# First layer in two stages with the norms inside, and the attention half of the joined scan stage issued by steps for all batches

## The reference

```python
# _layernorm: (x - mean) / sqrt(var + 1e-5)
x = x + L0_attn(_layernorm(x))        # layer 0
#   h = layernorm(x)*g1 + b1; q,k,v = h@wq, h@wk, h@wv; phi = elu + 1
#   kv = sum_s phi(k) v ; z = sum_s phi(k)
#   x = x + (phi(q) kv / (phi(q) z + 1e-6)) @ wo
#   h = layernorm(x)*g2 + b2
#   x = x + lookup(h @ w1) @ w2
#   lookup(u) = gelu(0.1 * clip(round(10 u), -128, 127))
...
x = x + L1_attn(_layernorm(x))        # gated scan h = A*h + b, y = gate*h, y @ w_o + residual
x = x + L1_xattn(_layernorm(x), ctx)  # softmax(q k / sqrt(128)) v over 32 keys, no output projection
```

## Time and profile before

| what | value |
|---|---|
| median of 3 runs | 2153.41 us (2146.08 to 2165.81) |
| the profiled execution's own time | 2144.94 us |
| its span | 2143.2 us |
| PE (TensorE matmul) busy | 1911.1 us, 89% |
| DVE (VectorE) busy | 1396.5 us, 65% |
| ACT (ScalarE) busy | 1154.5 us, 54% |
| POOL (GpSimd) busy | 859.1 us, 40% |
| mean granted TensorE clock | 0.94 |

### The profile page before, as it was taken

How to read it: one execution, slowest core, us unless ns; L and a number is a source line. 1 busy time by engine, 2 the same in 40 slices (tenths; PEclk the granted TensorE clock), 3 DMA queues, 4 the chain that set the end, 5 groups by cost and what they waited for, 6 DMA issues and landing times. The chain is left out here.

```text
span 2143.2 us, 50870 instructions
## 1 busy us (share of the span) xinstructions
PE 1911.1 (89%) x20208; PEld 1368.9 (64%) x20208; DVE 1396.5 (65%) x2479; ACT 1154.5 (54%) x2435; POOL 859.1 (40%) x1107
## 2 busy tenths in 40 slices
PE   4888999988568999999999877999999989999786
PEld 2435787863345788888888753788778856633332
DVE  3655887864756677777766433788777768934434
ACT  3455555555567666566655434555555562056453
POOL 0002454520325576666665210566666640044200
PEclk8998999998668999999999988999999999989898
DMA  6000100000002200000000040444444420000100
GB/s 284 1 1 1 58 33 30 30 11 0 1 1 86 84 23 13 23 13 23 14 22 22 14 187 1 138 130 132 122 118 128 129 60 2 1 1 1 36 1 21
DMA packets 31951, 107.02 MB, mean 50 GB/s; under 512 B 9440, under 2 KB 9568, under 8 KB 30816
## 3 DMA queue, kind: packets, MB, share of 16 engines
q1 hardware_dynamic: 30624, 103.58, 14.6%
q10 hardware_dynamic: 1088, 0.13, 0.0%
HBM read 93.67 MB, written 10.03 MB: 48 GB/s over the span
## 5 line engine op out<-in xcount | busy, mean ns | idle before, releaser
L611 PE MATMUL bank<-yh,wl 128*128 128x512 f32 x640 | 253.9, 397 | 14.9 <-DVE yl L1486 6.8
L612 PE MATMUL bank<-yl,wh 128*128 128x512 f32 x640 | 252.5, 395 | 0.0
L613 PE MATMUL bank<-yh,wh 128*128 128x512 f32 x640 | 252.0, 394 | 0.0
L2053 DVE SCALAR_TENSOR_TENSOR big<-bank,pack,big 128x256 f32<-128x256 f32 (+2 forms) x384 | 182.2, 477 | 34.8 <-ACT mask L1975 17.2
L1539 DVE TENSOR_TENSOR hl<-bank,hh 128x512 fp32r<-128x512 f32 x192 | 132.8, 692 | 68.4 <-ACT hh L1476 59.0
L1974 ACT ACTIVATE big<-bank,pack 128x256 f32<-128x256 f32 x192 | 91.0, 474 | 133.6 <-PE bank L1809 133.2
L1476 ACT ACTIVATE hh<-bank 128x512 fp32r<-128x512 f32 x192 | 115.1, 599 | 84.4 <-DVE bank L1534 82.9
L611 PEld LDWEIGHTS bank<-yh,wl 128*128 128x128 f32 x640 | 122.1, 191 | 50.1 <-issue 14.6
L699 ACT ACTIVATE a<-bank,pack 128x512 f32<-128x512 f32 x128 | 88.1, 689 | 105.3 <-PE bank L613 105.3
L603 POOL CAST wh<-big 128x384 fp32r<-128x384 f32 x64 | 61.9, 966 | 197.3 <-PE bank L613 134.7
L613 PEld LDWEIGHTS bank<-yh,wh 128*128 128x128 f32 x640 | 122.1, 191 | 26.3
(11 more groups left out here) (497 smaller groups left out, 4661.1 us busy)
## 6 DMA issues: line engine op xcount, KB each, us to landing
rep<-routing SPq DMA_DIRECT2D x64, 384.0 KB, 3.4
rep<-routing SPq DMA_DIRECT2D x64, 256.0 KB, 3.9
big<-in_big SPq DMA_DIRECT2D x1, 9216.0 KB, 25.5
rep<-routing SPq DMA_DIRECT2D x16, 512.0 KB, 3.5
gate<-big SPq DMA_DIRECT2D x32, 256.0 KB, 2.0
z<-gate SPq DMA_DIRECT2D x16, 512.0 KB, 3.5
rep<-routing SPq DMA_DIRECT2D x64, 128.0 KB, 3.6
big<-in_big SPq DMA_DIRECT2D x1, 6144.0 KB, 34.5
```

Source lines behind the costliest of these rows:

```text
L611: nc.tensor.matmul(out, pl, dh[:, cur], start=start, stop=False)
L612: nc.tensor.matmul(out, ph, dl[:, cur], start=False, stop=False)
L613: return nc.tensor.matmul(out, ph, dh[:, cur], start=False, stop=stop)
L2053: ins = nc.vector.scalar_tensor_tensor(out=d, in0=conv_in(i, back), scalar=weight(i, 3 - back), in1=d, op0=ALU.mult, op1=ALU.add)
```

## The change

**Layer 0 becomes two stages.** `l0_attention` takes x and does both norms itself. The inner norm no longer goes through a ratio: since var of the normed row is v/(v+1e-5), both inverse roots come from the same variance v, as exp(-0.5 ln(v + 1e-5)) and exp(-0.5 ln(1.00001 v + 1e-10)). VectorE then needs three operations a batch where it had five. The norms of batches 0 and 1 are issued ahead of the loop, those of 2 and 3 inside its steps 0 and 1. The value bank is shared with the key-value state and the denominator bank with the output projection, so that the banks suffice; on TensorE the values are projected after keys and queries.

`l0_lookup_mlp` takes res and does its norm inside as well, interleaved with the first chunks. Rounding is `10 u + MAGIC` as before, but the limits are applied in the shifted range (`max(MAGIC-128)`, `min(MAGIC+127)`), ScalarE subtracts MAGIC (Identity with a bias) and Gelu takes the factor 0.1 as its scale. GpSimd adds res onto x at the stage's start, so VectorE's finish is one add. The down product lags four chunks.

**Layers 3 and 4.** The attention half is written by steps over all batches: centre and variance of pairs, queries and scores of pairs, one softmax for two batches (256 columns), transposes and outputs of pairs, in more banks.

```diff
-        norm(nc, k, x, y, 1e-5, inner=(1e-5, k.w["L0_attn_ln1_g"], k.w["L0_attn_ln1_b"], a))
-        l0_attention(nc, k, y, a, res)
-        norm(nc, k, res, y, 1e-5, scaled=(k.w["L0_attn_ln2_g"], k.w["L0_attn_ln2_b"]))
-        l0_lookup_mlp(nc, k, y, res, x)
+        l0_attention(nc, k, x, y, a, res)
+        l0_lookup_mlp(nc, k, res, y, x)
...
+            def invert(b):
+                r, t = rs[b % 2][:, :], ts[b % 2][:, :]
+                act.wait_ge(s["var"], b + 1)
+                after(act, s["y_ready"], b - 1)
+                nc.scalar.activation(t, var, ACT.Ln, scale=1.0 + 1e-5, bias=k.eps[1e-10]).then_inc(s["ln"], 1)
+                nc.scalar.activation(r, var, ACT.Ln, bias=k.eps[1e-5]).then_inc(s["ln"], 1)
+                act.wait_ge(s["ln"], 2 * b + 2)
+                nc.scalar.activation(t, t, ACT.Exp, scale=-0.5).then_inc(s["inv"], 1)
+                nc.scalar.activation(r, r, ACT.Exp, scale=-0.5).then_inc(s["inv"], 1)
...
+            centre(0)
+            variance(0)
+            centre(1)
+            variance(1)
             for b in range(B + 1):
                 if b < B:
...
+                    project_in(b)
                 if b:
...
+                    sums(b - 1)
+                if b + 2 < B:
+                    centre(b + 2)
                 if b < B:
...
+                    states(b)
+                if b + 2 < B:
+                    variance(b + 2)
                 if b:
...
+                    project_out(b - 1)
...
+            for i in range(N + 4):
+                if i < N:
+                    pe.wait_ge(s["h_ready"], i // C + 1)
+                    after(pe, s["rounded"], i - 2)
+                    nc.tensor.matmul(up_bank[i % 3], w1[:, sl(i % C, P)], y[:, sl(i // C)], start=True, stop=True).then_inc(s["up"], 1)
+                if i == 0:
+                    centre(2)
+                if i == 1:
+                    centre(3)
+                    variance(2)
+                if i == 2:
+                    variance(3)
+                if i >= 4:
+                    down(i - 4)
...
+            for i in range(N + 1):
+                if i < N:
+                    centred_grid(i)
+                if i == 1:
+                    square(2)
+                    invert(2)
+                    square(3)
+                    invert(3)
+                if i:
+                    act.wait_ge(s["grid"], i)
+                    after(act, s["down"], i - 4)
+                    nc.scalar.activation(g[(i - 1) % 4][:, :], r[(i - 1) % 4][:, :], ACT.Gelu_apprx_tanh, scale=0.1).then_inc(s["act"], 1)
...
-                link(nc.vector.tensor_scalar(rr, k.ps[i % 4][:, :], 10.0, MAGIC, ALU.mult, ALU.add))
-                link(nc.vector.tensor_scalar(rr, rr, MAGIC, -128.0, ALU.subtract, ALU.max))
-                nc.vector.tensor_scalar(rr, rr, 127.0, 0.1, ALU.min, ALU.mult).then_inc(s["grid"], 1)
...
+                    nc.vector.tensor_scalar(cur, cur, MAGIC - 128.0, MAGIC + 127.0, ALU.max, ALU.min).then_inc(s["limited"], 1)
```

More of the change, by code:

```diff
@@ L157, in _ @@
             for b in range(B + 1):
                 if b < B:
[L159 to L165, removed]
@@ L206, in _ @@
+            normed(0)
             for b in range(B + 2):
@@ L235, in l0_lookup_mlp @@
     C = 4
-    with ExitStack() as mem, stage(nc, "up rounded grid act down chain done") as (block, s):
+    N = B * C
+    names = "centred squared var ln inv h_ready added up rounded limited grid act down done chain"
+    with ExitStack() as mem, stage(nc, names) as (block, s):
         sb = lambda n, w: mem.enter_context(nc.sbuf_tensor(f"{n}_{nc.next_id()}", [P, w], F32))
-        r, g = sb("r", 3 * S), sb("g", 3 * S)
+        r, g = [sb("r", S) for _ in range(4)], [sb("g", S) for _ in range(4)]
+        sq, rs = ([sb(n, S) for _ in range(2)] for n in ("sq", "rs"))
@@ L239, in l0_lookup_mlp, with _, centre, variance @@
         w1, w2 = k.w["L0_attn_w1"], k.w["L0_attn_w2"]
+        xc, var, up_bank, down_bank = k.ps[0:2], k.ps[2], k.ps[3:6], k.ps[6:8]
+        @block.gpsimd
+        def _(pool):
+            for b in range(B):
+                nc.gpsimd.tensor_tensor(x[:, sl(b)], x[:, sl(b)], res[:, sl(b)], ALU.add).then_inc(s["added"], 1)
         @block.tensor
         def _(pe):
+            def centre(b):
+                after(pe, s["h_ready"], b - 1)
+                nc.tensor.matmul(xc[b % 2], k.w["centre"], res[:, sl(b)], start=True, stop=True).then_inc(s["centred"], 1)
+            def variance(b):
+                pe.wait_ge(s["squared"], b + 1)
+                after(pe, s["ln"], b)
+                nc.tensor.matmul(var, k.mean, sq[b % 2][:, :], start=True, stop=True).then_inc(s["var"], 1)
@@ new lines, in finish @@
+            def finish(b):
+                dve.wait_ge(s["down"], C * (b + 1))
+                dve.wait_ge(s["added"], b + 1)
+                nc.vector.tensor_tensor(x[:, sl(b)], x[:, sl(b)], down_bank[b % 2], ALU.add).then_inc(s["done"], 1)
+            normed(0)
+            for i in range(N + 1):
+                if i < N:
+                    dve.wait_ge(s["up"], i + 1)
+                    after(dve, s["act"], i - 3)
+                    nc.vector.tensor_scalar(r[i % 4][:, :], up_bank[i % 3], 10.0, MAGIC, ALU.mult, ALU.add).then_inc(s["rounded"], 1)
+                if i == 0:
+                    normed(1)
+                if i == 3:
+                    normed(2)
+                if i == 5:
+                    normed(3)
+                if i < N:
+                    cur = r[i % 4][:, :]
+                    dve.wait_ge(s["rounded"], i + 1)
+                    nc.vector.tensor_scalar(cur, cur, MAGIC - 128.0, MAGIC + 127.0, ALU.max, ALU.min).then_inc(s["limited"], 1)
+                if i % C == 2 and i > C:
+                    finish(i // C - 1)
```

365 lines of the change are left out of this document (218 added, 147 removed).

## The result

| | before | after |
|---|---|---|
| median | 2149.74 us (4 runs, 2143.49 to 2165.81) | 2115.82 us (4 runs, 2113.15 to 2120.99) |
| ratio | | 0.9852, 95% interval 0.9813 to 0.9891 |
| profiled span | 2143.2 us | 2113.0 us |
| layer 0, stage 1 (first matmul to last add) | 60.8 | 45.8 (forecast 47.0) |
| layer 0, stage 2 (the same) | 45.5 | 47.3 (forecast 44.7) |

The change saves 1.5% of the time, 33.9 us between the medians. The forecast was 2123 us, 7 us above the measured median.

What follows compares the result with a forecast made beforehand. No engine alone bounds the program; norm and layers 3 and 4 are chains, the latter slowed by the clock. 13.8 + 0.8 + 14.9 + 0.9 = 30.4 us off 2144.9 gives 2114.5, plus 8.5: 2123 us, range 2112 to 2132.

Steps and rivals of the forecast that it cites:

- Stage 1: Layer 0's first norm and attention: keys start at 22.1 instead of 36.74, last add at 59.6; gain 13.8 us.
- Stage 2: Layer 0's second norm and lookup MLP: first down product at +20.45, end at +44.7 against 45.5; gain 0.8 us.
- until about 26 us: Layer 0's attention, step 0: keys, queries, values at half clock until then; step 8.2 us; earlier rise gains up to 3.
- one add: End of the lookup MLP: last product's result at +44.0, then a single add to +44.7.
- Stage 3: Attention half of layers 3 and 4: last add at 530.15 instead of 545.0; gain 14.9 us.
- I keep the full clock: Attention half of layers 3 and 4: TensorE never idle over 1.3 us, so full rate; half the 14.9 us rests on it.
- The table load: Lookup MLP, before the first Gelu: now on the chain, 1.28 us, next activation 0.01 later, without the skill's 1.38 us drain.
- (a): Rival, attention half of layers 3 and 4: clock falls all the same, no gain there, 2138 us; chance 0.24 whole or part.
- (b): Rival: clock rises early in stage 1 and softmax is cheap, 3 + 2 us more, 2118 or less; chance 0.09.
- (c): Rival: TensorE at half rate through layer 0's two stages, 28 us slower, 2181; chance 0.04.
- (d): Rival: Identity and Gelu need different tables, 15 pairs of loads, 38 us; no chance of its own.
- GpSimd's adds: Start of the lookup MLP stage: four adds beside the norm's first 6 us, first needed at about +26, costing nothing before.

Runs made afterwards that it cites:

- the second profile: The changed kernel measured again, nothing altered: median 2118.11 us against 2153.87, ratio 0.983.
- only_layer0: Kernel before with only layer 0 changed to two stages, layers 3 and 4 as before: median 2133.40 us, ratio 0.990.
- late_finish: Changed kernel with VectorE's add of a finished batch moved behind chunk 3 instead of chunk 2 in the lookup MLP: one run, 2115.15 us.
- before_lean: Kernel before with 11 idle TensorE matmuls of 256 to 512 columns in the attention half of layers 3 and 4: one run, 2140.78 us.
- own_norm_late: Changed kernel with layer 0's second norm its own stage and the finished batch's add behind chunk 3: one run, 2111.20 us.
- own_norm: Changed kernel with layer 0's second norm as a stage of its own again: one run, 2127.55 us.
- only_scan: Kernel before with only the attention half of layers 3 and 4 by steps, layer 0 as before: median 2134.17 us, ratio 0.991.
- before_filled: Kernel before with 18 idle TensorE matmuls of 512 columns in the attention half of layers 3 and 4: median 2155.41 us, ratio 1.0006.

## Why the prediction was right, point by point

**The sum.** Forecast 13.8 + 0.8 + 14.9 + 0.9 = 30.4 us; the profiles give 15.0 - 1.8 + 15.0 + 0.8 for the same four terms, and 30.2 between the spans. The four measured terms make 29.0; the rest is the earlier start and some 1 us in stages that nobody touched. Stage 1 came out 1.2 better than forecast and stage 2 2.6 worse, and that the profiles agree to 0.2 us is luck. The time of 2123 us was 7.2 too high for another reason: the prediction added the 8.5 us by which the median lay above the profiled execution before, and in the changed kernel the median lies 1.0 above it (2115.82 against 2114.86).

**Stage 1.** The step "TensorE is what the first projection waits for: keys start at 22.1" was right to 0.2 us. The term mis-sized was the half clock "until about 26 us": it ended at about 23.6, which makes the first step 7.2 us instead of 8.2. That it was named as the stage's unknown was right; the second profile had it gone before the first key, and its first step took 6.7. That the two norm matmuls make step 1 the long one held (8.7).

**Stage 2.** "Gain 0.8 us" was wrong in sign: 1.8 us were lost. Two things are missing from the walk. The start: I took the norm of batch 0 at +7.2 as before, but the products ran at half rate for longer (3.75 us for the first two pairs, 3.30 in rows 5) and the first up product was at +8.2: 1.0 us. In another execution it was at +5.8, and in only_layer0 at +7.1. The end: I counted "one add" behind TensorE's last product and let the 27 products run without a gap, and did not ask what is queued behind VectorE's add of batch 2. late_finish measured it: 1.45 us. 44.7 + 1.0 + 1.45 is 47.15, against 47.3 measured. The statement that TensorE is the bound from the first down product on held but for that one wait: 0.86 us a product, VectorE busy 24.2 of 47.4 us.

**Stage 3.** Forecast last add 26.37 us after the first centre, measured 26.28. The clock term was the bold one: "I keep the full clock" held in every profile with the new list, and before_lean puts the clock at 8.1 or more of the 15.0, near the "half" of the text or somewhat above it. The softmax on 256 columns took 0.41 to 0.42 us an operation against 0.45 taken.

**The table load.** The row (1.28, next activation 0.01 later) was borne out at 78.08 in the new place, where it is on the path. The drain that the Trainium skill adds (ScalarE: Activation LUTs, section What ACT_TABLE_LOAD costs) does not show here either.

**The rivals.** (a) did not occur: the clock stayed up in the attention half in all nine profiles with the new list, and the half took 26.3 us in each. (b) occurred in part in the second profile of the changed kernel, where an early clock took 1.4 us off stage 1 (and 2.4 off stage 2, which (b) doesn't speak of); the softmax was not much cheaper. (c) and (d) did not: table loads number 26 in both kernels.

**GpSimd's adds.** "They lie beside the norm's first 6 us, where VectorE is idle" was right, and that cover is worth more than I said ("uncovered they would cost nothing before that date"). own_norm_late shows them beside VectorE: 0.82 and 0.35 us more on the first two limits.

## What to carry to other kernels

When a stage is a chain through three engines with a slow clock, pair the steps of independent batches: here it removed waits and at the same time kept TensorE's clock up, and the clock was half of the gain or somewhat more. When you walk a hand-written list, ask of every operation that waits (a batch's final add, above all) what stands behind it on its engine; one 0.69 us add in the wrong place cost 1.45 us. Interleaving a norm into the stage it feeds pays where the fill is otherwise empty (stage 1, 8.7 us of overlap) and not where it delays the date from which the bounding engine runs without a gap (stage 2: a norm of its own was 3.3 us shorter, once GpSimd's adds and the table load were out of the way too). Those 3.3 us were seen in the stage and not in the whole time.

## What the runs showed of the hardware that was not expected

**VectorE slows beside GpSimd, here only from SBUF.** A fp32 tensor_scalar from SBUF to SBUF took 1.25 and 0.78 us beside GpSimd's fp32 adds and 0.43 without (own_norm: 1.24 and 0.77 against 0.43); the same form from PSUM took 0.68 to 0.69 in both. In both runs the slowed operation ended 0.28 or 0.29 us after one of GpSimd's adds had ended, as if it had waited for that add. The Trainium skill (GPSIMD Engine Reference, section Specifications) has the SBUF interfaces as shared with VectorE, with contention for VectorE instructions in a two-port mode or with two SBUF inputs. These rows fit the first case; no run here shows which mode L373 runs in.

**Untouched stages scatter by 20 us with the clock.** From the start of the stage behind layers 3 and 4 to the end, the instructions are the same in all fourteen profiles, yet it took 1595.7 us in the shortest (own_norm_late) and 1616.0 in the longest (only_scan); over the whole execution the granted clock was 0.951 and 0.936. Two stretches of 80 us, 1200 and 1280 us behind that start, show the largest difference in clock. Of the six profiles above 1605 us, five have 0.77 to 0.83 in one or both of them, which no shorter one has; before_filled (1606.6) does not. The kernel before (1597.7 us), then only_scan:

```profile
1745.54:1825.54 80.00, 71.36 (x622) 44.95 (x622) 57.73 (x63) 27.50 (x40) 9.49 (x15) 0.96 0.00 1
1825.54:1905.54 80.00, 76.00 (x740) 44.72 (x736) 52.81 (x56) 19.72 (x31) 9.91 (x25) 0.91 0.00 1
```

```profile
1729.83:1809.83 80.00, 71.27 (x514) 45.23 (x524) 46.36 (x50) 25.70 (x37) 8.20 (x14) 0.79 0.00 1
1809.83:1889.83 80.00, 74.31 (x676) 49.72 (x680) 60.03 (x62) 8.48 (x13) 3.21 (x8) 0.81 0.00 1
```

The stretches lie at the same distance from the stage's start but don't hold the same instructions (622 matmuls in the first, 514 in the slower run). A busy share of about 0.9 on TensorE went with clock 0.96 in the one and 0.79 in the other, so the share alone doesn't tell the clock. The scatter is larger than most of the differences that the variants above make, and is why a gain of 7 us inside one stage could not be shown in the whole.
